# Keys and queries stacked on partitions by transfers: a head's scores in one matmul over 98 rows

## What is computed

```python
x = x + 0.5 * ffn(layernorm(x), weight, bias)
x = x + attention(layernorm(x), Wqkv, bqkv, Wo, bo)
x = x + 0.5 * ffn(layernorm(x), weight, bias)
# ffn: weights rounded to -1, 0, 1 times their mean magnitude, then one product
# attention, 16 heads of 32:
scores = einsum('bsnh,btnh->bnst', k, q) / sqrt(32)
scores = triu(scores) + -10000.0 * tril(ones, k=-1)
attn = softmax(scores, axis=2)
out = einsum('bnkq,bknh->bqnh', attn, v) @ Wo + bo
```

## Time and profile before

| | |
|---|---|
| median of 3 runs | 1117.07 us (1115.98 to 1118.72) |
| the profiled execution | 1115.44 us, its span 1113.7 us |
| TensorE, ScalarE, VectorE, GpSimd busy | 96%, 83%, 66%, 31% of the span |
| granted clock of TensorE, mean | 0.983 |
| share of the 16 DMA engines | 20.5% for the kernel's queue, 76 MB |

### The profile page before, as it was taken

How to read it: one execution, slowest core, us unless ns; L and a number is a source line. 1 busy time by engine, 2 the same in 40 slices (tenths; PEclk the granted TensorE clock), 3 DMA queues, 4 the chain that set the end, 5 groups by cost and what they waited for, 6 DMA issues and landing times.

```text
span 1113.7 us, 26124 instructions
## 1 busy us (share of the span) xinstructions
PE 1067.9 (96%) x9472; PEld 691.1 (62%) x9472; DVE 738.9 (66%) x2306; ACT 921.7 (83%) x2577; POOL 344.0 (31%) x471
## 2 busy tenths in 40 slices
PE   5799999999999999999999999999999999999896
PEld 3576656565666565665666666675666666665465
DVE  6866577787535767789644766789744667765344
ACT  2269998999989989889988988878988998999641
POOL 3841232233001313345201322435401322311343
PEclk8898999999999999999999999999999999998999
DMA  6463211021004110421112211421112212000121
GB/s 207 153 217 125 97 50 40 3 78 50 24 19 154 32 59 31 158 73 43 38 41 87 77 59 50 144 78 40 51 40 86 69 40 69 21 12 13 60 66 38
DMA packets 42015, 77.71 MB, mean 70 GB/s; under 512 B 5536, under 2 KB 11680, under 8 KB 41888
## 3 DMA queue, kind: packets, MB, share of 16 engines
q1 hardware_dynamic: 41888, 76.04, 20.5%
HBM read 49.81 MB, written 25.17 MB: 67 GB/s over the span
## 4 chain that ended last, share of the span: by engine, by line
PE 76%; ACT 11%; DVE 6%; issue 2%; POOL 2%; DMA 1%; SPq 0%; DVEq 0%; ACTq 0%; POOLq 0%
PE bank L1173 31%; PE bank L1294 10%; PE bank L1232 10%; PE bank L1266 10%; PE bank L1195 7%; ACT masked_scores L1073 6%; ACT prob L1099 4%; PE bank L1184 3%; PE bank L1274 3%; DVE masked_scores L909 2%; DVE st L859 1%; DMA xt<-in_L_attn_x_dram 1%; DVE hn L878 1%; POOL xt L769 1%; PE bank L1251 1%
## 5 line engine op out<-in xcount | busy, mean ns | idle before, releaser
L909 DVE CUSTOM_DVE_ANT_0 masked_scores<-bank,mask 128x512 f32<-128x512 f32 (+3 forms) x768 | 379.6, 554 | 221.3 <-PE bank L1232 220.2
L1073 ACT ACTIVATE masked_scores<-masked_scores,mst 128x512 f32<-128x512 f32 (+3 forms) x768 | 467.7, 620 | 2.9 <-DVE mst L909 2.9
L1099 ACT ACTIVATE prob<-bank 128x512 f32<-128x512 f32 (+1 forms) x640 | 302.0, 559 | 58.5 <-PE bank L1274 57.4
L1173 PE MATMUL bank<-hT,wqk 128*128 128x512 f32 x768 | 190.9, 397 | 0.0
L808 POOL TENSOR_SCALAR_AFFINE_SELECT prob<-prob 128x512 f32<-128x512 f32 (+1 forms) x96 | 78.6, 819 | 346.5 <-ACT prob L1099 345.8
L1266 PE MATMUL bank<-qT,kT 32*128 32x512 f32 (+2 forms) x2304 | 169.6, 378 | 4.5 <-DVE kT L886 1.6
L1232 PEld LDWEIGHTS bank<-kT,qT 32*128 32x128 f32 x2304 | 94.4, 185 | 115.6 <-issue 52.8
L1232 PE MATMUL bank<-kT,qT 32*128 32x512 f32 (+2 forms) x2304 | 161.2, 377 | 3.4 <-ACT prob L1099 2.6
L1173 PEld LDWEIGHTS bank<-hT,wqk 128*128 128x128 f32 x768 | 140.4, 188 | 37.9 <-ACT prob L1099 8.2
L1073 ACT ACTIVATION_READ_ACCUMULATOR masked_scores<-masked_scores,mst 128x1 f32 x768 | 156.4, 204 | 0.0
L1266 PEld LDWEIGHTS bank<-qT,kT 32*128 32x128 f32 x2304 | 97.7, 185 | 70.4 <-issue 48.4
(11 more groups left out here) (87 smaller groups left out, 971.7 us busy)
## 6 DMA issues: line engine op xcount, KB each, us to landing
wqk<-weight_scratch SPq DMA_DIRECT2D x30, 512.0 KB, 3.4
wvo<-weight_scratch SPq DMA_DIRECT2D x20, 512.0 KB, 6.0
xt<-in_L_attn_x_dram SPq DMA_DIRECT2D x32, 256.0 KB, 4.2
residual_scratch<-xt SPq DMA_DIRECT2D x32, 256.0 KB, 2.0
xt<-residual_scratch SPq DMA_DIRECT2D x32, 256.0 KB, 3.1
out_dram<-xt SPq DMA_DIRECT2D x32, 256.0 KB, 2.0
o<-in_L_attn_Wqkv_dram SPq DMA_DIRECT2D x12, 256.0 KB, 4.7
weight_scratch<-o SPq DMA_DIRECT2D x6, 512.0 KB, 3.0
```

Source lines behind the costliest of these rows:

```text
L909: nc.vector.tensor_tensor_reduce(masked_scores[:, h, at:at + n], psum(u, h)[:, at:at + n], mask[:, off:off + n], -SCALE, BIG, ALU.add, ALU ...
L1073: nc.scalar.activation(of, of, ACT.Exp, bias=mst[:, c + kc, to:to + 1], scale=-1.0, accum_out=ssum[:, c + kc, to:to + 1]).then_inc(a_free, 1)
L1099: nc.scalar.activation(prob[:, at % 2, h, off:CW], psum(("S", b, n), h)[:, off:CW], ACT.Exp, scale=SCALE)\
L1173: m = nc.tensor.matmul(psum(u), left(x, k), right(y, k), start=(n == 0), stop=(n == len(terms) - 1))
```

## The change

What it does:

- The order of a group's projections is K0, Q0, Q1, K1. They stand in slots 8, 9 (K0 and Q0 of the group after next) and 1, 2 (Q1 and K1 of the next group; slots 2 and 4 in `GROUP3_ROWS`), where they stood in slots 9, 0, 1 and 2 (9, 0, 3 and 4 in `GROUP3_ROWS`). Feed-forwards and transposes are moved by a slot to fit.
- A projection is evacuated into one buffer `stage` (HI and LO). From there SyncE issues 12 transfers (`stack`): for each of the four heads three of 32 partitions by 512 elements, so that a head's keys lie as HI, LO, HI on partitions 0 to 95 (`kst`) and its queries as HI, HI, LO (`qst`), each of the two in a ring of three pieces. The transfers of a piece stand in the slot behind the projection, or in the slot where the piece they overwrite was last read (K1: slot 6).
- Partitions 96 and 97 of the keys hold ones, those of the queries the rows of the maxima. A head's scores are one matmul over 98 rows (two where two key blocks share a bank), its block of maxima one over 96 for each tile of queries. The loop over heads is outermost, and TensorE signals each head by itself.
- ScalarE waits, before the high part of a projection, until the 12 transfers of the projection before have landed. TensorE waits for the stacks ahead of a block of maxima.
- `masked_scores` has 2 buffers where it had 4, `prob` 6 where it had 8. ScalarE does the exponentials of heads 0 and 1, then the old block's last sum, then heads 2 and 3. The mask on the diagonal is two instructions where the four heads wrap round the ring of six.

Its core:

```diff
-    second = (Q_, K_) if g == 0 else (K_, Q_)
-    return [("P", b, g, K_, 0), ("P", b, g, Q_, 0)] + [("P", b, g, j, 1) for j in second]
+    return [("P", b, g, K_, 0), ("P", b, g, Q_, 0), ("P", b, g, Q_, 1), ("P", b, g, K_, 1)]
...
-    "T3.2 F2.1 | A | X3.5",
-    "F2.2 P | A",
+    "F2.1 P | A | X3.5",
+    "T3.2 P | A",
 )
 GROUP1_ROWS = (
-    "C T3.3 P | A | X3.6",
+    "C T3.3 F2.2 | A | X3.6",
...
-    "M T1.6 F1.5 | A",
-    "T2.2 T1.7 F1.6 | A",
-    "T2.3 F1.7 | A",
-    "T2.4 P | A",
+    "M T2.2 T1.6 F1.5 | A",
+    "T2.3 T1.7 F1.6 | A",
+    "T2.4 F1.7 P | A",
+    "T2.5 P | A",
...
+NPIECE, NPROB = 3, 6
+STACK, ROWS = 3 * HD, 3 * HD + 2
+
+
+def piece(u):
+
+    n = 2 * (u[1] * GROUPS + u[2]) + u[4]
+    return n % NPIECE, n // NPIECE + 1
+
+
+def outlived(u):
+
+    n = 2 * (u[1] * GROUPS + u[2]) + u[4] - NPIECE
+    if n < 0:
+        return None
+    last = (6, 9) if u[3] == K_ else (2, 9)
+    return n // 2 * STEPS + last[n % 2]
...
+MOVES = [[] for _ in SLOTS]
+for at, s in enumerate(SLOTS):
+    for u in s.uses():
+        if u[0] == "P":
+            old = outlived(u)
+            MOVES[at + 1 if old is None else max(at + 1, SLOT_OF[old])].append(u)
...
-        kT = [sb(f"kT{n}", [P, 2, S], F32R) for n in range(2)]
-        qT = sb("qT", [P, 3, 2, CW], F32R)
-        mneg = sb("mneg", [P, CHUNKS, CW], F32R)
-        prob = sb("prob", [P, 2, 4, CW])
+
+        kst = [sb(f"kst{n}", [P, 4, CW], F32R) for n in range(NPIECE)]
+        qst = [sb(f"qst{n}", [P, 4, CW], F32R) for n in range(NPIECE)]
+        stage = sb("stage", [P, 2, CW], F32R)
+        prob = sb("prob", [P, NPROB, CW])
         o = sb("o", [P, NO, CW])
-        masked_scores = sb("masked_scores", [P, 4, CW])
-        rall = sb("rall", [8, CW], F32R)
+        masked_scores = sb("masked_scores", [P, 2, CW])
+        rows_of = sb("rows_of", [P, CW], F32R)
...
+        def stacked(u):
+
+            n, times = piece(u)
+            return (kst_in if u[3] == K_ else qst_in)[n], 192 * times
+
+        def place(n, h):
+
+            return (4 * n + h) % NPROB
...
-                    sp.dma_start(mneg[part:P:HD, c, :].bitcast(F32), mrow[:, c, part, :].bitcast(F32))\
+                    at = slice(STACK + part, STACK + part + 1)
+                    sp.dma_start(queries_of(b, g, c)[at, :, :].bitcast(F32), mrow[:, part, :].bitcast(F32))\
                         .then_inc(mrow_in[c], 16)
+
+            def stack(u):
+
+                sp.wait_ge(ring_free, freed(u))
+                if outlived(u) is not None:
+                    sp.wait_ge(s_full, 4 * outlived(u) + 4)
+                n, _ = piece(u)
+                to, parts = (kst[n], (HI, LO, HI)) if u[3] == K_ else (qst[n], (HI, HI, LO))
+                for j, part in enumerate(parts):
+                    for h in range(4):
+                        sp.dma_start(to[HD * j:HD * j + HD, h, :].bitcast(F32), stage[HD * h:HD * h + HD, part, :].bitcast(F32))\
+                            .then_inc((kst_in if u[3] == K_ else qst_in)[n], 16)
...
+                for u in MOVES[k]:
+                    stack(u)
...
-                dve.wait_ge(ring_full, full(u))
                 for h in range(4):
-                    if EARLIER[u] is not None:
-                        dve.wait_ge(a_free, block_at(EARLIER[u], h))
+                    dve.wait_ge(ring_full, full(u) - 3 + h)
+                    if h >= 2:
+                        dve.wait_ge(a_free, block_at(u, h - 2))
+                    elif EARLIER[u] is not None:
+                        dve.wait_ge(a_free, block_at(EARLIER[u], h + 2))
                     for j, r, at, n, off in block_tiles(u):
                         to = 4 * h + r
-                        nc.vector.tensor_tensor_reduce(masked_scores[:, h, at:at + n], psum(u, h)[:, at:at + n],
+                        nc.vector.tensor_tensor_reduce(masked_scores[:, h % 2, at:at + n], psum(u, h)[:, at:at + n],
...
+                    low(u, stage[:, LO, :], psum(u), stage[:, HI, :], (bias_of(u[3], u[2]), ALU.add))
...
+                    at = PROJECTIONS.index(u)
+                    if at:
+                        act.wait_ge(*stacked(PROJECTIONS[at - 1]))
+                    i = nc.scalar.activation(stage[:, HI, :], psum(u), ACT.Identity, bias=bias_of(u[3], u[2]))
...
-            def exponentials(b, n):
+            def exponentials(b, n, heads):
                 off = live(n % STEPS)
                 at = step(b, n)
-                for h in range(4):
-                    nc.scalar.activation(prob[:, at % 2, h, off:CW], psum(("S", b, n), h)[:, off:CW], ACT.Exp, scale=SCALE)\
+                for h in heads:
+                    act.wait_ge(s_full, 4 * at + h + 1)
+                    if 4 * at + h >= NPROB:
+                        act.wait_ge(value_done, (4 * at + h - NPROB) // 4 + 1)
+                    nc.scalar.activation(prob[:, place(at, h), off:CW], psum(("S", b, n), h)[:, off:CW], ACT.Exp, scale=SCALE)\
                         .then_inc(s_exp, 1)
...
-                    act.wait_ge(s_full, step(b, s.step) + 1)
-                    if step(b, s.step) >= 2:
-                        act.wait_ge(value_done, step(b, s.step) - 1)
-                    exponentials(b, s.step)
+                    exponentials(b, s.step, (0, 1))
                 if k and SLOTS[k - 1].blocks:
                     block_sums(SLOTS[k - 1].blocks[-1], (3,))
+                if s.step is not None:
+                    exponentials(b, s.step, (2, 3))
...
-                    pe.wait_ge(ring_free, freed(("P", b, g, Q_, c)))
-                    if kc:
-                        pe.wait_ge(ring_free, freed(("P", b, g, K_, kc)))
-                    for term, (x, y) in enumerate(((HI, HI), (LO, HI), (HI, LO))):
+                    pe.wait_ge(*stacked(("P", b, g, Q_, c)))
+                    pe.wait_ge(*stacked(("P", b, g, K_, kc)))
+                    for h in range(4):
+                        bank_free(u, h)
                         for j, r, at, keys, _ in block_tiles(u):
                             n = max(HALF, keys)
-                            for h in range(4):
-                                if term == 0 and j == 0:
-                                    bank_free(u, h)
-                                row = slice(HD * h, HD * h + HD)
-                                m = nc.tensor.matmul(psum(u, h)[:, at:at + n], query_piece(b, g, c)[row, x, P * r:P * r + P],
-                                                     kT[g % 2][row, y, CW * kc:CW * kc + n], start=(term == 0 and j == 0),
-                                                     stop=(term == 2 and j == len(u[5]) - 1))
-                    m.then_inc(ring_full, 1)
+                            m = nc.tensor.matmul(psum(u, h)[:, at:at + n], queries_of(b, g, c)[0:STACK, h, P * r:P * r + P],
+                                                 keys_of(b, g, kc)[0:STACK, h, 0:n], start=(j == 0), stop=(j == len(u[5]) - 1))
+                        m.then_inc(ring_full, 1)
...
-                for term, (x, y) in enumerate(((HI, HI), (LO, HI), (HI, LO))):
-                    for kb, off, at in parts:
-                        for h in range(4):
-                            if term == 0 and kb == keys[0]:
-                                bank_free(u, h)
-                            row = slice(HD * h, HD * h + HD)
-                            nc.tensor.matmul(psum(u, h)[:, at:at + CW - off], kT[g % 2][row, x, P * kb:P * kb + P],
-                                             query_piece(b, g, c)[row, y, off:CW], start=(term == 0 and kb == keys[0]),
-                                             stop=False)
                 if keys[0] == 0:
                     pe.wait_ge(mrow_in[c], 32 * group(b, g))
-                for kb, off, at in parts:
-                    for h in range(4):
-                        row = slice(HD * h, HD * h + 2)
-                        m = nc.tensor.matmul(psum(u, h)[:, at:at + CW - off], onesr[row, :], mneg[row, c, off:CW],
-                                             start=False, stop=(kb == keys[-1]))
-                m.then_inc(s_full, 1)
+                for h in range(4):
+                    bank_free(u, h)
+                    for kb, off, at in parts:
+                        key = P * (kb % QPC)
+                        m = nc.tensor.matmul(psum(u, h)[:, at:at + CW - off], keys_of(b, g, kb // QPC)[0:ROWS, h, key:key + P],
+                                             queries_of(b, g, c)[0:ROWS, h, off:CW], start=(kb == keys[0]), stop=(kb == keys[-1]))
+                    m.then_inc(s_full, 1)
```

131 lines of the change are left out of this document (69 added, 62 removed).

## The result

| | before | after |
|---|---|---|
| median of 4 runs each | 1117.88 us (1115.98 to 1118.72) | 1403.07 us (1400.5 to 1404.72) |
| ratio | | 1.2552, 95% interval 1.2525 to 1.2579 |
| span of the profiled execution | 1113.7 us | 1398.7 us |
| mean granted clock | 0.983 | 0.885 |

The change costs 285 us, where 35 were forecast. The direction was right, the size was outside the range.

A forecast was written before the change was run, and what follows sets the result against it. TensorE's own sequence was taken to bound plain groups (nine of sixteen), ScalarE five, VectorE two. Terms -18 + 28 + 10 + 12 + 3 = +35 us on the 1117.07 us median gave 1152 us, 8-in-10 range 1092 to 1190.

The forecast's parts named there:

- TensorE's part: Full matmuls replacing packed ones: scores and products before scores gain 26 us, 18 after discounting groups where ScalarE binds.
- The end of 0.58: Rival: each stacking transfer takes 0.58 us to issue, like the two-dimensional form; about 1240 us, chance 0.10.
- First and second place: TensorE waits for Q0's stack at slot 1, 28 us; ScalarE's stops around Q1, K1 in slots 1 and 2, 10.
- Third place: Program head: first group's projections wait for transfers in turn, so the first scores come late; 12 us lost.
- Fourth place: With two `masked_scores` buffers, VectorE's third head waits for ScalarE's first sum; 3 us lost, ends 0 to 12.
- The rival that gave this 30 us in plain groups: VectorE and ScalarE in step also bind plain groups, 0.5 us a slot in 60 slots; 1180 us, chance 0.12.
- (1): Sign on TensorE: full scores matmuls 0.23 us apart, slots without a stall about 0.15 shorter.
- (2): Sign on SyncE: a stacking transfer's issue at 0.33 us and twelve in 4.4.
- (3): Sign on ScalarE: projections wait for a stack transfer 1.5 to 1.9 us in about 20 places.
- (4): Sign on TensorE: waits for the transfers before blocks of maxima, 4 us where slot 0 is short.
- (5): Sign at the program's head: first scores about 11 us later than 99.95.
- the transfers stay hidden: Rival: twelve issues take about 2 us, so `stage` is held less than any slot; 1098 us, chance 0.22.

The follow-up runs named there:

- e13_two_queues: The changed kernel, whole and exact, with each piece's twelve transfers split six and six between SyncE and GpSimd; 1286.01 us.
- e11_table_before: The kernel before, its slot table and four `masked_scores` buffers, with the new scores and maxima matmuls on constant, never filled stacks; 1120.69 us, ratio 1.0016.
- e8_no_stack: The changed kernel with one transfer of 64 KB a piece instead of twelve, the rest of the stacks held constant; 1174.69 us.
- e5_two_buffers: The kernel before with two `masked_scores` buffers instead of four, nothing else changed; 1180.72 us, ratio 1.0574.
- e12: e9_four without its one transfer and without waits for it, in the changed table of slots; 1128.36 us.
- e10_three_quarter: The changed kernel with three transfers a piece instead of twelve, a quarter of the columns, the rest of the stacks constant; 1179.96 us in one run.
- e9_four: e8_no_stack with four `masked_scores` buffers and the waits of before, one key stack standing for three; 1132.64 us.

## Why the prediction was wrong

By its own steps, in their order, after the sizes. The forecast was 250 us short. e13_two_queues splits this best, because its transfers land 5.9 us behind the first issue, which is the 6.0 that I had forecast. So the wrong price of an issue is worth 1403 - 1286 = 117 us. At the landing time that I had forecast, the stops cost 1286 - 1175 = 111 us, where my three places had 28 + 10 + 12 = 50: 61 us more, for the way in which a stop passes through and for the clock (what GpSimd's own lateness adds in that kernel is in it). The two buffers add 39 to their 3, TensorE's part with what else is in e11_table_before 21, the table 8 and the one transfer that e8_no_stack keeps 4. Together 250. Of what the prediction says of the kernel before, all stands but one reading of the earlier trace rows, in the next paragraph.

**TensorE's part, forecast 18 us gained: measured none.** The scores' term was right to the hundredth (1.02 against 1.14). The step that failed is "block of maxima, 0.90 against 0.90". The single starts in the two traces show what the block is made of. Its twelve matmuls of 32 rows start in three sets of four, 0.34 and 0.23 us apart, and the product starts 0.33 behind the last set (365.38, 365.72, 365.95 and 366.28, the slot of the earlier trace rows): three passes of the array and 0.10 us for a change of array shape at each end. Four full ones start 0.34, 0.24 and 0.24 apart and the product follows 0.23 behind: four passes and the change in front alone, 1.05. Up to the reciprocals' row it is the packed block that pays at one end only, 0.82, and the full one at both, 1.12. I took 0.90 for bare passes and set the new block at four of them, 4 x 0.226, without the change in front that it keeps; my bound of 0.1 either way was below the 0.15 to 0.30 that came.

Over the 160 slots (median start to start, times count): 44 blocks of 512 columns at +0.15, 30 before the reciprocals' row at +0.30, 16 before transposes at +0.01, 29 of 384 at +0.07, 18 of 256 at +0.13, with the few others +22 us; and +8 for the small uses behind them (the reciprocals' row 0.43 against 0.31, and the transposes of maxima and sums), which I had not priced. Against this stand 19 us from the scores (95 at 0.12, 32 at 0.12, 32 at 0.10), 11 from 107 products before scores at 0.10 and 3 from 35 feed-forwards at 0.09, for which my 0.07 x 150 = 10 was near. So 30 us are lost and 33 gained: from 339.7 to 974.7 the kernel before takes 635.0 us, e11_table_before 633.4 for the same groups. The Trainium skill's 3.07 ("TensorE: Matmul & The Clock Gate", measured speedup vs the span model) agrees with the trace for the packed block, 0.88 us as an estimate against 0.82 to 0.90 measured; no row of the kernel before has the new block's 1.05 to 1.12.

**The transfers, forecast 7.6 us for `stage`: 10.5 to 11.8.** The price of an issue was the largest single error: 0.37 taken, 0.59 measured, on a pitch of 0.63. The end of 0.58 was among my bounds, with 1240 us as its time and 0.10 as its chance; I went by the wrong one of two rows, that of a plain transfer of 128 rows to memory, and not by that of the rows form that also writes from SBUF to SBUF. Landing (2.0 against 1.9) and evacuation were right. To it comes what SyncE has queued ahead: Q1's transfers were ready at 460.4 and began at 461.76, behind 3.2 us of issues for the two rows' pairs and a weight load. I had counted no queue. The Trainium skill's "usually small" for the time to initiate a DMA ("DMA: Bandwidth & Descriptors", issuing engines are not separate DMA queues) holds here for one issue, 0.59 us before 2.0 of landing, and not for twelve in a row, 7.5 before the same 2.0. In the plain group the hold of K0 is 10.5 us, from 431.85, where ScalarE's part of its evacuation starts, to 442.39, and that of Q1, from 458.98 to 470.74, 11.8.

**First and second place, forecast 38 us.** Most of the 228 us of the transfers is here: 27 of them fall to the head, as first scores at 133.4 in after and 106.8 in e8_no_stack show, and some 200 to the groups. (Two slips of adding don't matter beside this: the stops that I list for the second place make 15.9 us and not 15.5, and the 15 group changes of the first have 14 terms.) There are three causes:
- The hold. Both places grow with it. My own rival had this right in kind, but with 0.58 an issue it gave 1240 us, and 1403 came.
- How a stop passes through. This step failed at any price of an issue. I sent ScalarE's stop to TensorE by way of the exponentials and the bank of head 2's scores, a part of it lost on the way, and at slot 0 not at all. The trace shows a shorter way: the bank that the waiting projection lies in is itself the third that the next block of maxima wants. The stop arrives nearly whole in slots 0 and 3 (4.35 and 5.58 us of ScalarE's 5.42 and 6.12), and makes 121.3 us of waits over the span. It could have been counted in the code: a ring of seven, four for the scores, two for the block's first heads, and the next is the projection's.
- The clock. I wrote that I saw no cause for the granted clock to change. Behind the stops of 3.5 to 5.6 us, three in the plain group, it was 0.50 for a while: 0.87 on the mean in the group where it was 1.00, and by the estimate above at most 68 us in all.

**Third place, the head: 12 forecast, 33.4 measured, 27 of it with the transfers.** The first scores start at 133.4 instead of 99.95. The first block of maxima waits until 82.11, 13.8 us later than at 68.28 where I had 7.7, again two holds in a row; then it goes on at the lower clock, and the second pair of pieces costs another 7.3 and 5.8:

```profile
82.11 2.07 PE L1298 MATMUL bank<-kst,qst 96*128 96x256 f32 x8 [13.21 <-DMA qst<-stage]
...
103.90 1.65 PE L1298 MATMUL bank<-kst,qst 96*128 96x512 f32 x3 [7.34 <-DMA qst<-stage]
...
131.28 1.79 PE L1298 MATMUL bank<-kst,qst 96*128 96x384 f32 x3 [5.83 <-DVE stage L952]
```

**Fourth place, VectorE and ScalarE in step: 3 forecast, ends 0 to 12; measured 42 beside the other parts, 64 alone.** The step that failed is the argument from slack: "VectorE has 18 us of slack in 60". That slack did not hide a wait that falls in nearly every slot between two engines that take turns. The rival that gave this 30 us in plain groups was close: the nine plain groups grow by 25 us in e5_two_buffers, and the other seven by 38.

**What was left out.** The new table costs 8 us on its own (e12 against e11). I had priced the moved projection only by what it waits for, not by the uneven slots that it leaves.

The parts that the runs separate, each as the difference of two medians: transfers 1403 - 1175 = 228; buffers 1175 - 1133 = 42; the last transfer 4; the table 1128 - 1121 = 8; TensorE's products and the rest 3. Together the 285. The 4 and the 3 are within what a measurement can tell. Of the signs that I had named, (1) came half true: full matmuls start 0.23 us apart, and slots without a stall are 0.2 shorter or 0.2 longer; (2) came out as 0.59 and 7.5 us, (3) as 29 waits of 5.8 us on the mean and not 20 of 1.5 to 1.9, (4) as 3.5 us in slot 1 of the plain group and two longer stops, in slots 0 and 3, that I had no sign for, (5) as 33 us and not 11. The "prediction is wrong if (2) is" that I wrote thought only of the cheaper side.

The rival "the transfers stay hidden", 1098 us with a chance of 0.22, would have been wrong with nearly hidden transfers as well: e10_three_quarter and e8_no_stack come nearest to that, and stand at 1180 and 1175. No version of these beats the kernel before; the nearest, e11_table_before, equals it with the transfers left out. What stays open is how much of the 200 us in the groups is clock and how much stop (68 us is an estimate of the most, not a measurement), and whether a second `stage` buffer would let the transfers hide: the changed kernel has no room for one (e9_four gave up two key stacks for buffers of that size), and it was not tried.

## What to carry to other kernels

A step that hands a buffer on by DMA holds it for evacuation + (count of transfers x issue time) + landing, and the price of the issue has to come from a row of the same form and direction; where two forms in the trace differ by 1.7 times and the count is twelve, that choice is the forecast. When an in-order engine stops, ask first which bank or buffer the unfinished piece itself occupies and who needs it next, before following longer ways. And compare packed matmuls with full ones by passes of the array plus a change of shape at each end where the neighbour has another shape, read from the single starts: four heads packed in rows were already as cheap as stacked ones.
